# A decoder layer on one core: rope tables that carry the heads' factors, a root's square on ScalarE, and a new order of work

## What is computed

```python
q = rms(x @ Wq.T + bq); k = rms(x @ Wk.T + bk); v = x @ Wv.T + bv   # 16 heads of 16, 4 key heads
q = rope(q) * q_gain;   k = rope(k)                                 # rope: cos and sin by position
x = layernorm(x + softmax(causal(q * HD**-0.5 @ k.T)) @ v @ Wo.T + bo)
x = layernorm(x + wkv(time_decay, time_first, x, ctx))              # a recurrence over 128 steps
h = relu(x @ sign(up).T * up_scale)
x = layernorm(x + h @ sign(down).T * down_scale * output_scale)
```

## Time and profile before

| | |
|---|---|
| median of 3 runs | 180.86 us (180.26 to 181.03) |
| the profiled execution | 180.35 us, its span 178.6 us |
| busy: DVE, PE, ACT, POOL | 161.1, 156.2, 136.1, 89.8 us |

### The profile page before, as it was taken

The page is one execution under the profiler, slowest core; times in us unless marked ns, Lnnn a source line. Parts: engine busy times, 40 slices in busy tenths (PEclk is TensorE's granted clock), DMA queues, the critical chain, the costliest instruction groups (busy, mean ns, idle before and its releaser), DMA issues.

```text
span 178.6 us, 3840 instructions
## 1 busy us (share of the span) xinstructions
PE 156.2 (87%) x1388; PEld 107.2 (60%) x1388; DVE 161.1 (90%) x296; ACT 136.1 (76%) x271; POOL 89.8 (50%) x111
## 2 busy tenths in 40 slices
PE   7999486988998999999999999997979697999740
PEld 2454242554644555667875579767767585898630
DVE  1589999869999979999999999999999999998973
ACT  3744795897787789999899998695599696799700
POOL 8227755046314284073995485644966156230542
PEclk9999999999999999999999999999999999999997
DMA  5999460060510880202580100000400100011203
GB/s 173 245 327 402 165 147 4 2 148 2 95 51 4 205 208 6 59 4 45 117 194 18 43 6 0 4 0 0 176 0 4 59 0 0 4 76 44 109 17 121
DMA packets 17989, 14.65 MB, mean 82 GB/s; under 512 B 12656, under 2 KB 13616, under 8 KB 17712
## 3 DMA queue, kind: packets, MB, share of 16 engines
q1 hardware_dynamic: 17424, 13.87, 27.2%
q10 hardware_dynamic: 544, 0.50, 0.8%
HBM read 9.52 MB, written 2.10 MB: 65 GB/s over the span
## 4 chain that ended last, share of the span: by engine, by line
DVE 41%; PE 35%; issue 12%; ACT 4%; DMA 3%; POOL 2%; DVEq 1%; POOLq 0%; SPq 0%
PE banks L582 10%; PE banks L566 7%; DVE state L1675 5%; PE banks L490 4%; DVE stats L1649 4%; PE banks L523 4%; DVE rot L1599 3%; DVE hid_lo L1733 3%; DMA probs<-biases_dram 3%; DVE rope_b L1585 3%; DVE banks L1592 2%; PE banks L462 2%; PE banks L500 2%; PE banks L509 2%; ACT probs L947 2%
## 5 line engine op out<-in xcount | busy, mean ns | idle before, releaser
L947 ACT ACTIVATE probs<-banks 128x1024 f32<-128x1024 f32 x32 | 32.1, 1024 | 7.0 <-PE banks L469 4.9
L566 PE MATMUL banks<-x2hi,up_sb 128*128 128x256 f16 x128 | 29.1, 273 | 2.3 <-DVE x2lo L1726 2.2
L582 PE MATMUL banks<-dn_sb,hid_hi 128*128 128x256 bf16 x128 | 29.3, 272 | 2.2 <-DVE hid_lo L1733 2.0
L582 PE MATMUL banks<-dn_sb,hid_lo 128*128 128x256 bf16 x128 | 29.2, 273 | 0.0
L566 PE MATMUL banks<-x2lo,up_sb 128*128 128x256 f16 x128 | 29.1, 273 | 0.0
L407 PE MATMUL banks<-wqkv_sb,xT_sb 128*128 128x384 f32 x64 | 22.9, 501 | 2.3 <-ACT probs L947 2.3
L995 ACT ACTIVATE banks<-banks,ups_man 128x256 f32<-128x256 f32 x48 | 19.6, 453 | 3.2 <-PE banks L566 3.0
L1332 POOL TENSOR_TENSOR qn<-rot,rscale 128x640 f32<-128x640 f32 x7 | 10.9, 1555 | 19.2 <-DVE rscale L1570 15.4
L407 PEld LDWEIGHTS banks<-wqkv_sb,xT_sb 128*128 128x128 f32 x64 | 12.2, 196 | 11.0 <-ACT probs L947 3.9
L1675 DVE TENSOR_TENSOR_SCAN state<-dec_sb,ke 128x1032 f32<-128x1032 f32 x8 | 18.4, 2305 | 0.3 <-POOL ke L1353 0.2
L1325 POOL TENSOR_TENSOR rstd<-veps,half_neg 128x2 f32<-128x2 f32 x24 | 17.3, 724 | 1.4
(11 more groups left out here) (124 smaller groups left out, 364.5 us busy)
## 6 DMA issues: line engine op xcount, KB each, us to landing
x_sb<-x_dram SPq DMA_DIRECT2D x8, 256.0 KB, 3.8
ctxT_sb<-ctxT_dram SPq DMA_DIRECT2D x8, 256.0 KB, 3.1
out_dram<-outb SPq DMA_DIRECT2D x8, 256.0 KB, 2.0
xT_sb<-xT_dram SPq DMA_DIRECT2D x7, 256.0 KB, 4.9
up_f<-up_dram SPq DMA_DIRECT2D x1, 1024.0 KB, 6.4
dn_f<-down_dram SPq DMA_DIRECT2D x1, 1024.0 KB, 8.4
wqkv_sb<-wqkv_dram ACTq DMA_DIRECT2D x2, 192.0 KB, 3.2
xT_sb<-xT_dram SPq DMA_DIRECT2D x2, 128.0 KB, 2.9
```

The lines of the kernel that those rows point to most:

```text
L566: mm = nc.tensor.matmul(banks[:, UP[p][n], s * T * S:(s + 1) * T * S], up_sb[:, c, j * 128:(j + 1) * 128], part[:, c, :, :].rearrange("p t ...
L582: mm = nc.tensor.matmul(banks[:, DN[p], t * D:(t + 1) * D], part[:, j, t * S:(t + 1) * S], dn_sb[:, j, :], start=(j == 0 and t == 0 and m ...
L947: nc.scalar.activation(probs[:, (T * p + t) % PROBS_N, 2 * h:2 * h + 2].rearrange("p n j s -> p n (j s)"), banks[:, b:b + 2], ACT.Exp).the ...
```

## The change

The factor of each head (its gain, 1/4 and -0.5) moves from the end of `newton_rms` into the rope tables: `rope_tables()` on GpSimd builds `cos_g` and `sin_g` (128x320 each) at the start, from `gain_b` and the tables of cosines and sines. The square `ysq` is computed on ScalarE (`first_square`). So DVE's `newton_rms` has two instructions in place of four. `split_out_biases` moves to GpSimd and `down_weights` to ScalarE. `ON`, the tables of banks and the order of all five lists are new; so is the place of `guard_tables()` in GpSimd's list. (`WHOLE` is empty, so the code that asks for it does what it did.) In the diff the first two new functions are on ScalarE, the third on GpSimd.

```diff
+        cos_g = sb("cos_g", [128, NQK, HD])
+        sin_g = sb("sin_g", [128, NQK, HD])
...
-            qn_done="GGGGGVGG",
-            hi_done="GGGAAAGA",
-            stack_done="AAAAAVVA",
-            kv_done="VGGVGVGG",
-            newt_done="GVVGGGGV",
-            guess_done="VVGGVVVG",
+            qn_done="VGVVGGGG",
+            hi_done="GGGAGGGA",
+            lo_done="GVVGVVGG",
+            stack_done="AVVVVVVA",
+            kv_done="VGGVGGGG",
+            newt_done="GVGVGGVV",
+            guess_done="GVVVVVGG",
             lo2_done="GGGVGGVG",
-            r3_done="GGGVVVGV")
+            r3_done="GGGGVVGV")
...
+            def down_weights():
+                act.wait_ge(dn_signs, 1)
+                act.wait_ge(small_ready, SMALL)
+                for j in range(NJ):
+                    nc.scalar.activation(down_of(j), dn_f[:, j], ACT.Copy, scale=ups_pow[:, j:j + 1]).then_inc(dn_ready, 1)
...
+            def first_square(p):
+                done(act, "y0_done", p)
+                nc.scalar.activation(ysq[:], y0[:], ACT.Square).then_inc(sems["ysq_done"], 1)
...
+            def rope_tables():
+                pool.wait_ge(rope_in, ROPE_IN)
+                pool.wait_ge(gain_ready, 2)
+                for to, of in ((sin_g, sin_sb), (cos_g, cos_sb)):
+                    nc.gpsimd.tensor_tensor(to[:], of[:].unsqueeze(1).to_broadcast([128, NQK, HD]),
+                                            gain_b[:].unsqueeze(2).to_broadcast([128, NQK, HD]), ALU.mult)\
+                        .then_inc(tables_ready, 1)
...
+            rope_tables()
+            split_out_biases()
             half_identity()
-            guard_tables()
-            scale_heads(0)
             high_heads(0)
             low_heads(0)
+            guard_tables()
             scale_heads(1)
             high_heads(1)
...
             def newton_rms(p):
-                done(dve, "y0_done", p)
-                nc.vector.tensor_tensor(ysq[:], y0[:], y0[:], ALU.mult).then_inc(signal("ysq_done", p), 1)
                 done(dve, "ysq_done", p)
                 nc.vector.scalar_tensor_tensor(vy[:], ssum[:], RMS_EPS, ysq[:], ALU.add, ALU.mult)
                 done(dve, "vy_done", p)
-                nc.vector.scalar_tensor_tensor(ny0[:], vy[:], 3.0, y0[:], ALU.subtract, ALU.mult)
-                done(dve, "ny0_done", p)
-                nc.vector.tensor_tensor(rscale[:, p % RSC_N], ny0[:], gain_b[:].rearrange("p t h -> p (t h)"), ALU.mult)
+                nc.vector.scalar_tensor_tensor(rscale[:, p % RSC_N], vy[:], 3.0, y0[:], ALU.subtract, ALU.mult)
```

More of the change, by code:

```diff
@@ L573, in ffn_down @@
             def ffn_down(p, n):
-                done(pe, f"hi{n}_done", p)
-                done(pe, f"lo{n}_done", p)
+                if n in WHOLE:
+                    done(pe, "hid_done", p, 2 * n + 2)
+                else:
+                    done(pe, f"hi{n}_done", p)
+                    done(pe, f"lo{n}_done", p)
                 if p == 0 and n == 0:
                     pe.wait_ge(dn_ready, NJ)
-                for j in (2 * n, 2 * n + 1):
+                for s in range(2):
+                    j = 2 * n + s
                     for t in range(T):
-                        for m, part in enumerate((hid_hi, hid_lo)):
-                            mm = nc.tensor.matmul(banks[:, DN[p], t * D:(t + 1) * D], part[:, j, t * S:(t + 1) * S],
-                                                  dn_sb[:, j, :], start=(j == 0 and t == 0 and m == 0),
-                                                  stop=(j == NJ - 1 and t == T - 1 and m == 1))
+                        parts = [hidden(p, n)[:, s]] if n in WHOLE else [hid_hi[:, j], hid_lo[:, j]]
+                        for m, part in enumerate(parts):
+                            mm = nc.tensor.matmul(banks[:, DN[p], t * D:(t + 1) * D], part[:, t * S:(t + 1) * S],
+                                                  down_of(j), start=(j == 0 and t == 0 and m == 0),
+                                                  stop=(j == NJ - 1 and t == T - 1 and m == len(parts) - 1))
                 mm.then_inc(sems["dn_mm"], 1)
@@ L694, in from_scores @@
                 attention_to_tokens(4, 0)
+                done(pe, "ek_done", 2)
+                done(pe, "probs_done", 5, 2)
+                scores(5, 1, guarded)
                 attention_to_tokens(4, 1)
@@ L1018, in _ @@
             first_root(0)
+            first_square(0)
+            decay_rates()
+            squares(1)
             take_values(1)
-            squares(1)
-            done(act, "ssum_done", 1)
+            mean_log(1)
+            take_values(2)
             squares(2)
-            mean_log(1)
+            swap_keys(0)
             first_root(1)
-            take_values(2)
-            decay_rates()
-            swap_keys(0)
+            take_values(3)
+            first_square(1)
             first_rows_out()
@@ L1207, in _ @@
             relu(5, 0)
-            high_bits(4, 2)
+            relu(5, 1)
+            done(act, "lo2_done", 4)
+            relu(5, 2)
             done(act, "dn_mm", 4, 1)
@@ L1616, in scale_heads, with low_heads @@
                                         .to_broadcast([128, T * NQK, HD]), ALU.mult).then_inc(signal("qn_done", p), 1)
+            def low_heads(p):
+                done(dve, "hi_done", p)
+                heads = stack[:, p % STACK_N, 0:T * HB].rearrange("p b g r d -> p (b g) r d")
+                nc.vector.tensor_tensor(heads[:, :, 1], qn[:, p % QN_N], heads[:, :, 0], ALU.subtract)\
+                    .then_inc(signal("lo_done", p), 1)
             def swap_keys(p):
@@ L1753, in _ @@
             rope_cosines(0)
+            rope_sum(0)
             newton_rms(0)
-            rope_sum(0)
-            done(dve, "rot_done", 0)
+            scale_heads(0)
             rope_sines(1)
-            done(dve, "rscale_done", 0)
             head_sums(1)
@@ L1794, in _ @@
             head_sums(4)
+            scale_heads(3)
+            small_constants()
             newton_rms(4)
             residual(0)
-            moments(0, 0)
+            done(dve, "rscale_done", 4)
+            head_sums(5)
             with dve.If(guarded):
                 row_maxima(2)
-            done(dve, "rscale_done", 4)
-            head_sums(5)
+            moments(0, 0)
             rope_sines(5)
+            attend_norm(1)
             rope_cosines(5)
+            rope_sum(5)
             normed(0, 0)
-            attend_norm(1)
-            rope_sum(5)
+            low_heads(4)
+            swap_keys(3)
             newton_rms(5)
-            scale_heads(5)
             keys_by_context(0)
@@ L1814, in _ @@
                 row_maxima(3)
+            moments(0, 1)
             rope_sines(6)
+            swap_keys(4)
             rope_cosines(6)
@@ L1818, in _ @@
             rope_sum(6)
-            num_by_rec(0)
+            done(dve, "rscale_done", 5)
             head_sums(6)
+            low_heads(5)
             refine(0)
-            swap_keys(5)
-            newton_rms(6)
-            moments(0, 1)
             residual(2)
+            moments(0, 2)
             with dve.If(guarded):
                 row_maxima(4)
+            newton_rms(6)
+            normed(0, 1)
+            swap_keys(5)
             done(dve, "rscale_done", 6)
             head_sums(7)
-            moments(0, 2)
-            normed(0, 1)
             add_mixed(0)
```

600 lines of the change are left out of this document (299 added, 301 removed).

## The result

The changed kernel takes 191.36 us (median of 4 runs, 190.08 to 193.08), the kernel before beside it 180.76. The ratio is 1.057, with a 95% interval of 1.053 to 1.061: 5.7% slower, 10.6 us between the medians. Slower was forecast, but 187.8, and the time lies above the range. The profiled execution took 191.59 us, its span is 189.7.

What follows compares the result with a forecast made beforehand. DVE, hardly ever idle, was taken as the bound, with PE full between 60 and 120 us. 180.35 + 9.5 (to first scores) - 1.1 - 1.1 = 187.65, given as 187.8 us; range 184.0 to 190.8.

Steps and rivals of the forecast that it cites:

- the wait for the guard tables: At the start: guard tables end at 18.0, so PE's project(2) begins at about 19.3 instead of 11.55, +7.7 us.
- the clock at the start: PE's idle gap drops the clock to half, so project(2)'s passes take +2.2 us, bounds 0 and 2.6.
- to scan(0): From first scores to scan(0): lighter DVE work against down weights on ScalarE, net -1.1 us; scan(0) at about 57.9.
- From scan(0) on: From scan(0) to the end: less DVE work and some idle time won, -1.1 us, bounds -3.7 and +1.
- The shared port: DVE held during POOL's instructions: six new two-input instructions exposed, 0 to 8 us possible; nothing added to the sum.
- DVE's work, -4.2: DVE's instructions over the whole kernel: 10.0 us gone, 6.5 taken over, about 0.7 less besides, net -4.2 us.
- the likeliest (184.6): Rival: the wait is there, but the clock stays up or the start is caught up further; 184.6 us, chance 0.14.
- The fourth: Rival: worse, through down weights showing in full, DVE-POOL collisions or late ScalarE squares; 191.5 us, chance 0.08.

Runs made afterwards that it cites:

- e1: Changed kernel with guard_tables() moved back ahead of the out bias and pair 0's heads in GpSimd's list: 181.93 us, ratio 1.006.
- e2: Kernel before with guard_tables() moved behind low_heads(0) in GpSimd's list: 191.23 us, ratio 1.058.
- e3: Changed kernel with 26 matmuls on zeros filling PE's wait ahead of the read of the flag: 188.28 us, ratio 1.044.
- e10: e6 plus the out bias on GpSimd behind half_identity, down weights left on DVE: 179.33 us, ratio 0.988.
- e13: e9 with normed(2, 0) moved behind residual(7) and normed(0, 7) behind low_x2(4) in DVE's order: 178.01 us, ratio 0.990.
- e15: Changed kernel, late guard tables kept, with the same two normed lines moved as in e13: 189.56 us, ratio 1.047.
- e9: e5 with the key swaps of pairs 3 and 4 back on ScalarE: 180.49 us, ratio 1.000.
- e14: e13 with three more DVE lines (low_heads(5), normed(0, 1), normed(0, 5)) moved off POOL's large instructions: 179.40 us, ratio 0.992.
- e5: Changed kernel with the guard's mask built behind the memsets and the identity's cast ahead of the rope tables: 180.56 us, ratio 1.000.
- e8: e5 with four and seven matmuls on zeros in two late waits of PE: 180.71 us, ratio 1.000.
- e12: e5 with the down weights back on DVE behind small_constants: 181.54 us, ratio 1.005.
- e4: Kernel before with only the rope tables, the square on ScalarE and two Newton instructions, old order kept: 179.82 us, ratio 0.996.
- e6: e4 with the guard's mask built behind the memsets and the identity's cast ahead of the rope tables: 178.83 us, ratio 0.989.
- e11: e10 with newton_rms(4) on DVE moved behind residual(0) and moments(0, 0): 180.42 us, ratio 0.997.

## Why the prediction was right and wrong

**Right: the wait for the guard tables, and the clock at the start.** End of the tables 18.0 (18.2 measured), project(2) at 19.3 (19.31), its passes +2.2 us (4.89 against 2.74), scores at 29.5 (29.23). e1, e2 and e3 show that this is the cause, not only a thing that happened. That project(2) came out to 0.01 us is luck: the tables ended 0.2 later, and from their end to the first matmul it took 1.1 us, where the sum took 1.3 though its working gave 1.1. The price of the clock held too, but was not read where the text says: in the stretch of the earlier trace rows the profile shows a granted clock of 1.00, although the passes were slow. The changed kernel has the price at 0.50: passes of 0.85 us, 0.64 apart. The ratio falls from 1.057 to 1.000 with the wait hidden.

**A little off: to scan(0).** Forecast at 57.9, measured 56.61: the start is made up for by 1.3 us more than I walked out (+7.1 in place of +8.4). The down weights took 3.29 us (3.3 to 3.8 forecast), and keys(0) came late behind them: DVE waited 1.24 us for it just ahead of scan(0). Which part of the walk gave the 1.3 us more is not shown.

**The step that failed: "From scan(0) on", -1.1, bounds -3.7 and +1.** Measured +4.0, outside its bounds. With the start 1.3 better and this 5.1 worse, the sum comes out 3.8 too low, which is the miss: 187.65 against 191.59 for the profiled execution. The step behind it is the one beside it, **"The shared port"**, which I left "at the means". I counted only new instructions with two SBUF inputs, six. Those lost little: qn stays at 0.82 us, the four low_heads went to 0.91, 0.3 us in all. The runs show that three other forms are held too: 16-bit copies (0.19 to 1.31 us each), TENSOR_SCALAR with a scalar per partition (0.73 to 1.7 us a pair) and its 16-bit output form (0.34 to 1.49 us each, e10). The change put eight more copies on DVE, and above all moved all lists, so that the pairs of `normed`, which DVE had before, met POOL's large instructions between scans 5 and 7, where before they did not (elsewhere in the kernel before single ones are held too, up to 1.38 us). The Trainium skill (SBUF — State Buffer, Who interferes with whom) names copies, casts and tensor_scalar among what can take the shared pair; the traces agree, with the numbers just given, and I had taken only two inputs from it. That the list is nearly the same there was no ground for "no loss there". Nor was any of DVE's idle time won, as the -1.1 assumed: it grew by 1.6 us.

Of the +4.0, e13 and e15 show 1.7 to 1.8 to be two pairs of `normed` between scans 5 and 6, by moving these alone; from scan(5) to the end e13 needs 60.45 us, the kernel before 60.41. Ahead of scan(1) the interval shrinks with the copies gone, but the median doesn't follow (e9), and freeing DVE further gives nothing (e14): that part is stretched instructions in the profile of the changed kernel, while what it is worth in the median is not shown. How often the second copy is held stays open: it is in the profiled executions of the changed kernel, e5 and e15, and is not in those of e1, e3, e8 and e12.

**DVE's work, -4.2.** Measured -1.3 in busy time. The count of instructions was right (15 fewer), and in the old order the tables and the square alone take 5.5 us away (e4). What came back are stretched instructions, about 3.0 us in 12 copies at 440 ns and 1.3 in 16 `normed` on x at 545 in place of 463. The new order also took holds away: two of the eight small `offset` instructions of the old one took 1.01 and 1.13 us beside POOL's 128x512 (before, at 114.25 and 149.51), and their sum fell by 1.9 us.

```profile
L1708 DVE TENSOR_SCALAR x<-r,stats,rstd 128x256 f32<-128x256 f32 x16 | 8.1, 545 | 0.1
...
L1668 DVE COPY stack<-stack 128x128 f16<-128x128 f16 x12 | 4.8, 440 | 0.0
```

**The rivals.** Of the likeliest (184.6) one half came: the start was caught up further, but the clock did fall. The fourth ("it is worse", 191.5, chance 0.08) named collisions with POOL among its three mishaps; they came, but in other instructions than the six that it named, and the other two did not show by scan(0), which came early. That its number lies next to 191.36 is luck. The range's upper end should have held it: the row that had shown a hold of 1.2 us stood for a kind of loss that a new order brings about anew, in instructions that were there before too.

**What is left of the change.** Its parts, each against its neighbour, from the ratios: place of the guard tables +5.7%; tables and square -1.1% (e6); out bias on POOL 0.0; new order +1.7% (1.2% by the medians), of which two lines are 1.0; down weights on ScalarE -0.5 in the new order, not clear of noise, +1.3 in the old one at the place that I gave them. Three versions are about 1.1% faster than before and lie within each other's intervals: e6, e10, and e13. The smallest edit of them is e6: tables, square and the guard mask built first.

## What to carry to other kernels

When a list is rearranged, walk first to the waits that an engine's *sequencer* makes (a flag, a branch): nothing of PE's list behind that wait started here, it showed as "issue" in the profile, and its price was three times that of the next term (5.7% against 1.7%). Then look at pairs of DVE and POOL that newly run at the same time: on DVE, copies and tensor-scalar instructions were as exposed here as two-input ones, and moving two lines by a few us of work was worth as much (1.0%) as the tables and the square (1.1%). Freeing an engine pays only to the next wait: e14 took 2 us off DVE and gave most of its step back where PE was full, and e11 filled one wait and met another.

## What the runs showed of the hardware

DVE's hold by POOL, by form, in these traces: a COPY of 128x128 f16 0.19 us free, 1.06 and 1.31 beside one 128x640 and one 128x512 instruction of POOL; a TENSOR_SCALAR of 128x256 f32 pair 0.73 free, 1.56 to 1.81 held; two `hid_lo` from `banks` (accumulator memory) took 1.28 together beside a 128x512 instruction of POOL that ran to 110.42 (e13, at 109.57), and a single one takes 0.67 to 0.69 us elsewhere, started 0.6 us apart; and the pair of TENSOR_SCALAR stayed at 0.73 beside POOL's 128x2 `rstd`.

The granted clock fell not only in the empty gap: in the changed kernel it is 0.50 in this stretch, ahead of which PE had waited 1.02 and 1.64 us between short groups of matmuls, and a pass of L578 went from 0.27 to 0.42 us:

```profile
143.00:149.00 6.00, 5.25 (x24) 3.62 (x25) 6.00 (x9) 4.46 (x11) 3.18 (x3) 0.50 0.01 3
```

With the clock held up there (e8) the time was the same within the intervals (1.000 both), with DVE busy without a gap: in this stretch the fall of the clock cost nothing that shows, while at the start, where all waited for PE, it cost 2.2 us (e3).
